# Scores of two heads in one ring slot, in the steps that have no tiles of maxima

## The chip, the cores and the metric

One core of a Trainium2 chip runs the whole program. The metric is the device time of one execution in microseconds (us), lower is better. A verdict compares runs of both kernels on the same chip.

## The reference

Eight sequences of 1024 tokens with 256 features pass through one transformer block: layer norm and modulation, attention with 16 heads of 16 features, then a feed-forward part with squared ReLU and a count of spikes over five steps. What matters here is the attention. Its scores pass through a softmax twice: first in blocks of 128 keys under a causal mask (a block that is wholly masked gives zeros), then, over all keys, on the results of the first.

```python
s = einsum('bhqd,bhkd->bhqk', q, k) / sqrt(16)
s = where(causal, s, -inf)                        # in blocks of 128 keys
e = exp(s - max(s, block));  probs = e / sum(e, block)   # masked blocks: 0
attn_probs = softmax(probs, axis=-1)              # over all 1024 keys
attn_out = einsum('bhqk,bhkd->bhqd', attn_probs, v)
```

## The kernel before

**Steps.** The scores are computed transposed, keys on the partitions. The lower triangle of key and query blocks of a head is cut into nine units of 512 columns (`UNITS`); a group of four heads passes through nine steps, one per unit, four groups make a batch of 36 steps, and 8 batches make 288 steps (`NUNIT`). Step n belongs to unit n % 9 and to place n % 36 of its batch. Units 1, 2 and 8 have two strips of keys, the others one.

**A step on TensorE** (`step` in the block of TensorE) goes through, in this order: the products with v of the unit seven steps back (line 799); the sums of e over a block of keys for the unit before (line 789); the spread of 1/sum over the partitions for the unit five steps back, in two ring slots (line 830); then the four heads' scores (lines 774 and 777, the second adds the causal mask), with other work put between them. In the steps of unit 0 the mixed products (lines 818 and 799) come ahead of the scores.

**Other work.** `FRONT` and `BACK` (and `FIRST`, `NEAR`, `LATE` at the ends) place the pieces of the next and the last batch by hand: transposes T1, T2 and AT (line 664), projections QK, V and O, the first feed-forward product F1 (line 719). `placed(n)` gives a step's two pieces; the first follows the first head's scores, the second the fourth head's. `QUANTA` places the second feed-forward product in quanta of two matmuls (line 731), in four places of a step. `tiles_of(n)` gives the tiles of block maxima (lines 749 and 752) of the next group: three in each step of units 1 to 6, none in those of units 7, 8 and 0, except at the very beginning. In unit 7 `turn_maxima` (line 762) transposes the maxima, and `outputs` (line 839) transposes the results of the group before.

**PSUM.** Four buffers take turns. Two score banks of 512 columns serve scores, pieces and the turned maxima in strict alternation (`score_slots`): whoever takes a bank waits until the one before it there has been read. Two ring slots of 1024 columns serve the spread 1/sums, the tiles of maxima and the outputs, alternating too (`RING_NO`): VectorE reads them all, and `ring_free` counts what it has freed.

**The other engines.** ScalarE takes each head's scores with one exponential of 512 columns (line 1042) into e, and five or six steps later takes the second exponential over 2048 columns (line 1047). VectorE multiplies e by the spread 1/sums, 1024 columns at a time (line 1181), takes maxima (line 1159) and splits them into two parts (lines 1173 and 1175), and does the layer norms' statistics (lines 1133 and 1139). GpSimd squares and splits. Each engine's order is written out; nothing is reordered at run time, and semaphores tie the engines together.

Of the kernel before, what the change touches and what calls it, by code (L numbers as in the profile page):

```python
# [54 lines left out]
LAG_R, LAG_E, LAG_P = 5, 6, 7  # L55
LAST = NUNIT + 14
# [7 lines left out]
for _h in range(QH):  # L64
# [17 lines left out]
FRONT = {(2, 1): ('T1', 0), (1, 0): ('T1', 1), (1, 1): ('T1', 2), (5, 0): ('T1', 3), (3, 1): ('QK', 0), (5, 1): ('QK', 1), (6, 0): ('QK', 2), (13, 0): ('QK', 3), (15, 0): ('QK', 4), (16, 1): ('QK', 5), (17, 0): ('QK', 6), (15, 1): ('V', 0), (19, 1): ('QK', 7), (24, 0): ('V', 1), (21, 1): ('V', 2), (29, 0): ('V', 3), (30, 0): ('BH', 0), (31, 0): ('BT', 0)}  # L82
BACK = {(8, 0): ('AT', 0), (8, 1): ('AT', 1), (9, 0): ('AT', 2), (12, 0): ('AT', 3), (10, 0): ('O', 0), (11, 0): ('O', 1), (12, 1): ('O', 2), (14, 0): ('O', 3), (18, 0): ('T2', 0), (18, 1): ('T2', 1), (20, 1): ('T2', 2), (24, 1): ('T2', 3), (19, 0): ('F1', 0), (20, 0): ('F1', 1), (21, 0): ('F1', 2), (23, 0): ('F1', 3), (26, 1): ('F1', 4), (27, 0): ('F1', 5), (27, 1): ('F1', 6), (28, 0): ('F1', 7), (32, 0): ('F1', 8), (32, 1): ('F1', 9), (33, 0): ('F1', 10), (35, 0): ('F1', 11), (38, 0): ('F1', 12), (39, 0): ('F1', 13), (40, 0): ('F1', 14), (40, 1): ('F1', 15)}
# [6 lines left out]
NEAR = {(39, 0): ("F1", 12), (39, 1): ("F1", 13), (41, 0): ("F1", 14), (41, 1): ("F1", 15)}  # L90
NEAR_QUANTA = {36: (0, 0, 0, 1), 37: (1, 1, 0, 1), 38: (2, 0, 3, 0), 42: (2, 2, 2, 2), 43: (2, 2, 2, 2)}
LATE = {(2, 0): ("AT", 0), (2, 1): ("AT", 1), (4, 0): ("O", 0), (4, 1): ("O", 1), (8, 0): ("AT", 2), (8, 1): ("AT", 3),
        (9, 0): ("T2", 0), (9, 1): ("T2", 1), (10, 0): ("O", 2), (10, 1): ("O", 3), (11, 0): ("F1", 0), (11, 1): ("F1", 1),
        (12, 0): ("F1", 2), (12, 1): ("F1", 3), (13, 0): ("F1", 4), (13, 1): ("F1", 5)}
# [4 lines left out]
    (2, 0): ("V", 0, 2), (2, 1): ("V", 0, 3), (6, 1): ("BH", 0, 0), (7, 1): ("BT", 0, 0),  # L99
    (10, 0): ("T1", 1, 0), (10, 1): ("T1", 1, 1), (11, 0): ("T1", 1, 2), (11, 1): ("T1", 1, 3),  # L100
# [16 lines left out]
def placed(n):  # L117

    out = [None, None]
    b, at = divmod(n, PERIOD)  # L120
    for k in range(2):
# [108 lines left out]

# [34 lines left out]

def score_slots():
# [3 lines left out]
    for n in range(LAST):  # L270
        p = placed(n)
        st = [("st", n, hh) for hh in range(QH)] if n < NUNIT else [None] * QH
        turn = ("turn", *turn_of(*turns(n))) if turns(n) else None
        begin = [p[0], st[0]] if piece_first(n) else [st[0], p[0]]
        steps.append([*begin, st[1], st[2], st[3], p[1], turn] if late_turn(n) else [*begin, st[1], turn, st[2], st[3], p[1]])
# [75 lines left out]
def build(nc, x, wqT, wkT, wvT, woT, bq, bk, bv, bo, wfcT, wprojT, cT, wmod, consts, out):  # L351
# [4 lines left out]
    with ExitStack() as ctx:  # L356
# [157 lines left out]

        block = ctx.enter_context(nc.Block())
# [3 lines left out]
        def _(sp):  # L519
# [18 lines left out]
            def load_stacks(g):  # L538
                b, f0 = g // NQ, QH * DK * (g % NQ)
                if g >= 2:  # L540
                    sp.wait_ge(st_ready, QH * NU * (g - 1))
# [101 lines left out]
        def _(pe):  # L643
# [32 lines left out]
            def piece(item):  # L676
# [25 lines left out]
                elif kind == "AT":  # L702
                    pe.wait_ge(ring_free, RING_NO["o", NQ * r + NQ - 1, n // NT if r == LB else 0] + 1)
# [61 lines left out]
            def scores(n, hh):  # L765
# [5 lines left out]
                slot = score_bank("st", n, hh)  # L771
# [6 lines left out]
                mm.then_inc(st_ready, 1)  # L778
# [101 lines left out]
            def step(n):  # L880
                first, second = placed(n)
# [13 lines left out]
                if piece_first(n) and first:  # L895
                    piece(first)
# [6 lines left out]
                if first and not piece_first(n):  # L903
                    piece(first)
                for item in single[0]:
                    quantum(n, *item)
                if n < NUNIT:
                    scores(n, 1)
                if turns(n) and not late_turn(n):
# [5 lines left out]
                if n < NUNIT:  # L915
                    scores(n, 2)
                if 1 in at:
# [7 lines left out]
                if second:  # L925
                    piece(second)
# [13 lines left out]
            def last_sums(c):  # L940

                pe.wait_ge(squared, 16 * LB + 4 * c + 4)
                pe.wait_ge(ring_free, len(RING_NO) - (1 if c == 0 else 0))
# [23 lines left out]
        def _(act):  # L967
# [68 lines left out]
            def first_exp(n, hh):  # L1036
# [4 lines left out]
                act.wait_ge(st_ready, QH * n + hh + 1)  # L1041
                act.activation(e[:, n % ES, hh, :], score[SCORE_SLOT["st", n, hh][0]][:, :], ACT.Exp, scale=DK ** -0.5).then_inc(e1_done, 1)  # L1042

            def second_exp(m):
                act.wait_ge(ring_free, RING_NO["r", m, 1] + 1)
# [9 lines left out]
            def sum_exp(t):  # L1055
                act.wait_ge(r_log, t + 1)
                act.activation(r_a[:, :], r_a[:, :], ACT.Exp, scale=-1.0).then_inc(r_exp, 1)

# [18 lines left out]
            def step(n):  # L1077
                b, s = divmod(n, PERIOD)
                first, second = placed(n)
# [8 lines left out]
                if piece_first(n) and first:  # L1088
                    take(first)
                if n < NUNIT:  # L1090
                    first_exp(n, 0)
                if first and not piece_first(n):
                    take(first)
                for item in sums_ended(n, 0):
                    take_sum(*item)
                if n < NUNIT:
                    first_exp(n, 1)
                if turns(n) and not late_turn(n):
                    take_turned(*turns(n))
                for item in sums_ended(n, 1):  # L1100
                    take_sum(*item)
                if n < NUNIT:
                    first_exp(n, 2)
                for item in sums_ended(n, 2):
                    take_sum(*item)
                if n < NUNIT:
                    first_exp(n, 3)
                if second:
                    take(second)
                for item in sums_ended(n, 3):  # L1110
                    take_sum(*item)
                if late_turn(n):
                    take_turned(*turns(n))
# [17 lines left out]
        def _(dve):  # L1131
# [34 lines left out]
            def split_maxima(g, k, blocks):  # L1166
# [3 lines left out]
                dve.wait_ge(ring_free, RING_NO["m", g, k] + 1)  # L1170
# [200 lines left out]
            def step(n):  # L1371
# [9 lines left out]
                first, second = placed(n)  # L1381
                if first and first[0] == "O":
                    take_output(first)
# [3 lines left out]
                if second and second[0] == "O":  # L1387
                    take_output(second)
# [177 lines left out]
```

## Time and profile before

| | |
|---|---|
| median of 3 runs | 2380.7 us (2380.19 to 2381.14) |
| the profiled execution | 2373.46 us |
| its span | 2371.6 us |
| TensorE, VectorE, ScalarE, GpSimd busy | 94%, 74%, 65%, 48% of the span |
| mean granted TensorE clock | 0.993 |

The span runs from the first instruction to the last; the rest of an execution's time lies around it. A busy share counts the time in which an engine has an instruction under way. TensorE's matmuls overlap: each is shown until its last result is written, some 0.16 us after the next has begun, so the starts of the instructions give their pace, and a wait that shows as idle time is about that much longer than shown. The releaser behind an idle time is the instruction whose semaphore ended it. The granted clock is the share of the full 2.4 GHz that TensorE got.

### The profile page before, as it was taken

The numbers are of one execution on the slowest core, as the hardware profiler recorded it, in microseconds if no ns is written. First come the engines' busy times: TensorE is split into PE (matmuls) and PEld (weight loads), VectorE is DVE, ScalarE is ACT, GpSimd is POOL, SyncE is SP. The second block draws the span as 40 slices with busy tenths as digits, with TensorE's granted clock in tenths as the row PEclk, the third lists the DMA queues.
The fourth block names the chain that finished last, engine by engine and source line by source line (L and its number), as shares of the span: only waits on it lengthen the run. The fifth ranks groups of instructions, "written<-read, shape, count | busy, mean of one in ns | idle before, by whom it ended". The sixth has DMA issues, their size and how long they took to land.

```text
span 2371.6 us, 46967 instructions
## 1 busy us (share of the span) xinstructions
PE 2220.5 (94%) x19324; PEld 1245.5 (53%) x19324; DVE 1750.9 (74%) x2113; ACT 1541.4 (65%) x2157; POOL 1137.5 (48%) x1070
## 2 busy tenths in 40 slices
PE   7889889999999999999999999999999999989988
PEld 4444344465545555455554555545554555545557
DVE  6787887768787676876778777776877767787456
ACT  2477676766667667675766766676666766667731
POOL 3153133545664456644666257653575544442630
PEclk8999999999999999999999999999999999999999
DMA  5233122211212113121133202231022211100000
GB/s 183 66 108 93 48 57 78 83 48 39 62 53 83 52 35 90 54 55 52 35 90 94 60 7 59 66 107 48 23 64 68 83 34 46 39 25 22 6 27 25
DMA packets 114066, 140.23 MB, mean 59 GB/s; under 512 B 8648, under 2 KB 86760, under 8 KB 113856
## 3 DMA queue, kind: packets, MB, share of 16 engines
q1 hardware_dynamic: 113856, 137.23, 20.4%
q8 instruction: 157, 2.57, 0.4%
q14 instruction: 53, 0.43, 0.1%
HBM read 74.26 MB, written 58.74 MB: 56 GB/s over the span
## 4 chain that ended last, share of the span: by engine, by line
PE 78%; DVE 9%; ACT 5%; POOL 4%; DMA 2%; issue 1%; SPq 0%; ACTq 0%; POOLq 0%
PE pv L799 11%; PE sums L789 9%; PE score L774 9%; PE ring L749 9%; PE score L719 8%; PE sums L731 8%; PE score L670 5%; PE score L687 4%; DVE e L1181 4%; PE ring L830 4%; DVE negmax L1159 3%; PE ring L752 2%; ACT e L1042 2%; PE score L777 2%; PE score L664 2%
## 5 line engine op out<-in xcount | busy, mean ns | idle before, releaser
L1042 ACT ACTIVATE e<-score 128x512 f32<-128x512 f32 x1152 | 672.2, 595 | 386.1 <-PE score L777 214.9
L1181 DVE TENSOR_TENSOR e<-ring,e 128x1024 f32<-128x1024 f32 x576 | 680.9, 1223 | 281.4 <-PE ring L830 281.0
L1159 DVE TENSOR_REDUCE negmax<-ring 128x8 f32<-128x1024 f32 x576 | 681.5, 1219 | 158.1 <-PE ring L752 147.2
L1047 ACT ACTIVATE e<-e 128x2048 f32<-128x2048 f32 x288 | 548.6, 1905 | 4.9 <-DVE e L1181 4.9
L774 PE MATMUL score<-q_st,k_st 112*128 112x512 bf16 (+3 forms) x1536 | 458.5, 330 | 56.3 <-ACT e L1042 23.7
L749 PE MATMUL ring<-k_st,q_st 96*128 96x512 bf16 (+3 forms) x1664 | 386.9, 317 | 38.8 <-DVE e L1181 18.4
L1486 POOL TENSOR_SCALAR r_p<-r_b,ab 128x256 bf16<-128x256 f32 x96 | 89.7, 934 | 548.7 <-DVE r_b L1187 548.7
L799 PE MATMUL pv<-e,v 128*17 128x512 f32 (+3 forms) x3072 | 311.4, 493 | 0.0
L789 PE MATMUL sums<-e,d_ones 128*32 128x256 f32 x4608 | 304.2, 382 | 1.5
L774 PEld LDWEIGHTS score<-q_st,k_st 112*128 112x128 bf16 x1536 | 147.8, 97 | 247.6 <-issue 120.7
L1465 POOL TENSOR_TENSOR gT<-gT 128x512 f32<-128x512 f32 x112 | 117.1, 1050 | 334.4 <-ACT gT L1015 334.4
L731 PE MATMUL sums<-w_proj,gT 128*128 128x256 f32 x896 | 259.4, 395 | 7.6 <-POOL gT L1465 3.7
L719 PE MATMUL score<-hT,w_fc 128*128 128x256 f32 x1024 | 244.3, 384 | 2.7 <-ACT e L1042 1.4
L789 PEld LDWEIGHTS sums<-e,d_ones 128*32 128x32 f32 x4608 | 147.3, 110 | 177.6 <-issue 92.2
L749 PEld LDWEIGHTS ring<-k_st,q_st 96*128 96x128 bf16 x1664 | 149.2, 98 | 146.3 <-DVE negmax L1159 42.2
L752 PE MATMUL ring<-mask_q,id_b 128*128 128x128 bf16 x1024 | 221.7, 221 | 0.0
L719 PEld LDWEIGHTS score<-hT,w_fc 128*128 128x128 f32 x1024 | 189.6, 190 | 33.3 <-ACT e L1042 6.3
L777 PE MATMUL score<-id_b,mask_q 128*128 128x128 bf16 x1024 | 192.3, 220 | 0.0
L731 PEld LDWEIGHTS sums<-w_proj,gT 128*128 128x128 f32 x896 | 148.4, 191 | 37.3 <-POOL gT L1465 6.5
L1477 POOL TENSOR_SCALAR below<-n 128x512 bf16<-128x512 f32 x104 | 154.9, 1490 | 7.4
L1015 ACT ACTIVATE gT<-score 128x512 f32<-128x512 f32 x112 | 66.9, 597 | 124.5 <-PE score L719 124.5
L752 PEld LDWEIGHTS ring<-mask_q,id_b 128*128 128x128 bf16 x1024 | 100.4, 98 | 53.3 <-issue 3.0
(148 smaller groups left out, 2600.2 us busy)
## 6 DMA issues: line engine op xcount, KB each, us to landing
q_st<-q_parts SPq DMA_DIRECT2D x31, 768.0 KB, 5.9
k_st<-k_parts SPq DMA_DIRECT2D x31, 768.0 KB, 8.7
q_parts<-qk_p SPq DMA_DIRECT2D x30, 384.0 KB, 2.6
k_parts<-qk_p SPq DMA_DIRECT2D x28, 384.0 KB, 2.6
x_in<-in_x SPq DMA_DIRECT2D x8, 1024.0 KB, 5.7
q_parts<-qk_p SPq DMA_DIRECT2D x30, 256.0 KB, 2.9
x_res<-in_x SPq DMA_DIRECT2D x30, 256.0 KB, 4.1
k_parts<-qk_p SPq DMA_DIRECT2D x28, 256.0 KB, 2.9
```

The lines of the kernel that those rows point to most:

```text
L719: mm = pe.matmul(ps[:, HALF * i:HALF * i + HALF], w_fc[:, k, P * f:P * f + P], (last_h if r == LB else hT2)[:, k, HALF * c:HALF * c + HALF ...
L731: mm = pe.matmul(sums[:, HALF:HALF + D], gT[:, f, P * i:P * i + P], w_proj[:, f, :], start=(n > NUNIT and f == 0), stop=(f == NF - 1), ski ...
L749: mm = pe.matmul(slot[:, c:stop], q, k_st[0:KROWS, g % 2, hh, c + shift:stop + shift], start=True, stop=not own, skip_group_check=True)
L752: mm = pe.matmul(slot[:, diag:diag + P], id_b[:, :], mask_q[:, :], start=False, stop=True, skip_group_check=True)
L774: mm = pe.matmul(slot[:, c:c + qb - qa], k_st[0:KROWS + MROWS, g % 2, hh, P * j:P * j + P], q_st[0:KROWS + MROWS, g % 2, hh, qa:qb], start ...
L777: mm = pe.matmul(slot[:, c:c + P], mask_q[:, :], id_b[:, :], start=False, stop=True, skip_group_check=True)
L789: mm = pe.matmul(sums[32 * hh:32 * hh + 32, 0:HALF], d_ones[:, 2 * TRI - 1 - row:2 * TRI + 31 - row], e[:, m % ES, hh, HALF * c:HALF * c + ...
L799: mm = pe.matmul(pv[32 * hh:32 * hh + VW, qa - at:qb - at], v1[:, b % 2, j, QH * g + hh, :], e[:, m % ES, hh, c:c + qb - qa], start=start, ...
L1042: act.activation(e[:, n % ES, hh, :], score[SCORE_SLOT["st", n, hh][0]][:, :], ACT.Exp, scale=DK ** -0.5).then_inc(e1_done, 1)
L1047: act.activation(v, v, ACT.Exp).then_inc(e2_done, 1)
L1159: dve.tensor_reduce(negmax[:, hh:hh + heads, at:at + NB // heads], slot[:, :].rearrange("p (h a n) -> p h a n", h=heads, n=P), AX_X, ALU.m ...
L1181: dve.tensor_tensor(v, ring[no % 2][:, :].rearrange("p (i n) -> p i n", i=2), v, ALU.mult).then_inc(ring_free, 1)
```

## The change

In the steps n for which `paired(n)` holds (units 0, 7 and 8, no tiles: 94 of the 288) the scores leave the score banks. They take two ring slots ("s", n, 0) and ("s", n, 1) behind the two of 1/sums, heads 0 and 1 in the halves of the first and heads 2 and 3 in those of the second, and ScalarE reads each slot with one exponential of 1024 columns. A ring slot whose last user were scores is waited for by `e1_done`, any other by `ring_free` as before, now counted by `FREE_NO` without the scores. The order within such a step is new: the first pieces and the first quanta go ahead of heads 0 and 1, the turned maxima and the middle quanta between the pairs, the rest behind. A step now has four places for pieces; what stood at the second place stands at the fourth in all tables, so other steps keep their order. `st_ready` counts only the other steps' scores (`ST_NO`), and SP's load of stacks waits by `scores_done`.

```diff
+PAIRED = (0, 7, 8)
...
+def paired(n):
+    return n % NU in PAIRED and n < NUNIT and not tiles_of(n)
...
     for _g, _k in tiles_of(_n):
         RING_NO["m", _g, _k] = len(RING_NO)
+    if paired(_n):
+        for _k in range(2):
+            RING_NO["s", _n, _k] = len(RING_NO)
     if turned_out(_n):
         RING_NO["o", turned_out(_n)[0], int(turned_out(_n)[1][0] > 0)] = len(RING_NO)
+RING_ITEM = list(RING_NO)
+FREE_NO = {item: k for k, item in enumerate(item for item in RING_ITEM if item[0] != "s")}
...
+        if paired(n):
+            steps.append([p[0], p[1], turn, p[2], p[3]])
+            continue
...
+        def scores_done(eng, n):
+            if paired(n):
+                eng.wait_ge(ring_ready, RING_NO["s", n, 1] + 1)
+            else:
+                eng.wait_ge(st_ready, ST_NO[n] + QH)
...
             def ring_slot(*item):
                 no = RING_NO[item]
-                if no >= 2:
-                    pe.wait_ge(ring_free, no - 1)
+                if no >= 2 and RING_ITEM[no - 2][0] == "s":
+                    _, n, pair = RING_ITEM[no - 2]
+                    pe.wait_ge(e1_done, QH * n + 2 * pair + 2)
+                elif no >= 2:
+                    pe.wait_ge(ring_free, FREE_NO[RING_ITEM[no - 2]] + 1)
                 return ring[no % 2]
...
-                slot = score_bank("st", n, hh)
+                if paired(n):
+                    if hh % 2 == 0:
+                        ring_slot("s", n, hh // 2)
+                    slot = ring[RING_NO["s", n, hh // 2] % 2][:, BANK * (hh % 2):BANK * (hh % 2) + BANK]
+                else:
+                    slot = score_bank("st", n, hh)
...
+                if paired(n):
+                    if p[1]:
+                        piece(p[1])
+                    for item in single[0]:
+                        quantum(n, *item)
+                    scores(n, 0)
+                    scores(n, 1)
+                    if turns(n):
+                        turn_maxima(*turns(n))
+                    for item in single[1]:
+                        quantum(n, *item)
+                    if p[2]:
+                        piece(p[2])
+                    for item in single[2]:
+                        quantum(n, *item)
+                    scores(n, 2)
+                    scores(n, 3)
+                    if p[3]:
+                        piece(p[3])
+                    if turned_out(n):
+                        outputs(*turned_out(n))
+                    for item in single[3]:
+                        quantum(n, *item)
+                    return
...
+            def paired_exp(n, pair):
+                if pair == 0:
+                    act.wait_ge(pv_done, blocks(n))
+                if pair == 0 and mixed(n):
+                    act.wait_ge(mixed_done, (n - LAG_P) // NU + 1)
+                no = RING_NO["s", n, pair]
+                act.wait_ge(ring_ready, no + 1)
+                act.activation(e[:, n % ES, 2 * pair:2 * pair + 2, :], ring[no % 2][:, :].rearrange("p (i n) -> p i n", i=2),
+                               ACT.Exp, scale=DK ** -0.5).then_inc(e1_done, 2)
...
+            def in_pairs(n, p):
+                for k in range(2):
+                    if p[k]:
+                        take(p[k])
+                for item in sums_ended(n, 0):
+                    take_sum(*item)
+                paired_exp(n, 0)
+                if turns(n):
+                    take_turned(*turns(n))
+                for item in sums_ended(n, 1):
+                    take_sum(*item)
+                if p[2]:
+                    take(p[2])
+                for item in sums_ended(n, 2):
+                    take_sum(*item)
+                paired_exp(n, 1)
+                if p[3]:
+                    take(p[3])
+                for item in sums_ended(n, 3):
+                    take_sum(*item)
```

## Rows read from the trace of the kernel before

**Rows 1.** The page, busy time, share of the span and instructions of an engine.

```profile
PE 2220.5 (94%) x19324; PEld 1245.5 (53%) x19324; DVE 1750.9 (74%) x2113; ACT 1541.4 (65%) x2157; POOL 1137.5 (48%) x1070
```

**Rows 2.** Groups by form: busy us, mean ns of one, idle us before with its releasers.

```profile
L1042 ACT ACTIVATE e<-score 128x512 f32<-128x512 f32 x1152 | 672.2, 595 | 386.1 <-PE score L777 214.9 <-PE score L774 148.7
L1047 ACT ACTIVATE e<-e 128x2048 f32<-128x2048 f32 x288 | 548.6, 1905 | 4.9 <-DVE e L1181 4.9
```

**Rows 3.** Windows: stretch, length, busy us of each engine, granted clock, DMA.

```profile
1208.72:1213.36 4.64, 4.64 (x37) 3.31 (x33) 3.00 (x3) 3.26 (x6) 4.29 (x6) 1.00 0.37 111
1215.55:1219.51 3.96, 3.96 (x34) 2.77 (x30) 2.35 (x2) 3.01 (x6) 0.00 (x0) 1.00 0.67 224
1221.27:1225.26 3.99, 3.37 (x30) 1.45 (x27) 3.11 (x4) 3.43 (x8) 0.57 (x1) 1.00 0.99 268
1276.15:1283.45 7.30, 4.94 (x32) 2.58 (x28) 5.24 (x15) 3.94 (x7) 2.52 (x3) 1.00 0.38 124
1285.65:1290.21 4.56, 3.54 (x24) 1.80 (x20) 4.33 (x9) 3.26 (x6) 2.85 (x3) 1.00 0.36 121
1292.31:1296.68 4.37, 3.69 (x33) 1.58 (x29) 3.26 (x5) 3.95 (x8) 4.37 (x4) 1.00 1.05 254
1345.86:1350.21 4.35, 4.28 (x34) 2.94 (x30) 2.66 (x3) 3.57 (x7) 0.00 (x0) 1.00 0.02 8
1352.41:1357.92 5.51, 5.51 (x39) 4.31 (x35) 2.36 (x2) 2.62 (x5) 0.00 (x0) 1.00 0.69 204
1359.67:1366.71 7.04, 6.20 (x40) 3.64 (x37) 3.11 (x4) 4.21 (x8) 3.42 (x6) 1.00 0.67 145
1419.49:1424.40 4.91, 4.29 (x34) 2.90 (x31) 4.16 (x13) 3.46 (x6) 4.65 (x4) 1.00 0.02 7
1426.59:1432.22 5.63, 5.44 (x37) 3.74 (x33) 5.39 (x8) 3.55 (x6) 5.38 (x5) 1.00 0.06 9
1433.97:1437.44 3.47, 2.83 (x27) 1.06 (x23) 3.27 (x4) 2.62 (x6) 3.31 (x4) 1.00 1.07 248
```

**Rows 4.** Timeline of VectorE: start, length, line, operation, tiles, count, idle before.

```profile
1209.16 2.56 DVE L1181 TENSOR_TENSOR e<-ring,e 128x1024 f32<-128x1024 f32 x2
...
1215.64 2.35 DVE L1181 TENSOR_TENSOR e<-ring,e 128x1024 f32<-128x1024 f32 x2 [1.10 <-PE ring L830]
...
1279.15 2.33 DVE L1181 TENSOR_TENSOR e<-ring,e 128x1024 f32<-128x1024 f32 x2
...
1345.96 2.56 DVE L1181 TENSOR_TENSOR e<-ring,e 128x1024 f32<-128x1024 f32 x2
...
1421.37 2.32 DVE L1181 TENSOR_TENSOR e<-ring,e 128x1024 f32<-128x1024 f32 x2
```

**Rows 5.** Timeline of TensorE, step 16 of the batch.

```profile
1276.44 0.38 PE L774 MATMUL score<-q_st,k_st 112*128 112x512 bf16 x1
...
1278.40 0.61 PE L762 MATMUL score<-id_b,maxp 128*64 128x128 bf16 x8 [1.52 <-DVE maxp L1175]
1278.93 0.39 PE L774 MATMUL score<-q_st,k_st 112*128 112x512 bf16 x1
...
1280.67 1.98 PE L687 MATMUL score<-hT,w_q 128*128 128x512 f32 x4
```

**Rows 6.** Timeline of TensorE, first scores of steps 9, 27 and 0.

```profile
1222.61 0.39 PE L774 MATMUL score<-q_st,k_st 112*128 112x512 bf16 x1
...
1362.36 0.39 PE L774 MATMUL score<-q_st,k_st 112*128 112x512 bf16 x1
...
1434.73 0.39 PE L774 MATMUL score<-q_st,k_st 112*128 112x512 bf16 x1
```

**Rows 7.** Timeline of TensorE, a tile of maxima in batch 7.

```profile
2113.71 0.23 PE L749 MATMUL ring<-k_st,q_st 96*128 96x128 bf16 x1 [1.91 <-DVE e L1181]
```

**Rows 8.** Windows of batch 7 and of the last steps.

```profile
2115.00:2121.00 6.00, 5.64 (x33) 1.76 (x31) 5.85 (x11) 2.69 (x3) 3.19 (x4) 0.50 0.00 0
2258.20:2261.40 3.20, 3.20 (x26) 0.94 (x24) 0.69 (x1) 0.00 (x0) 3.04 (x3) 0.50 0.00 0
```

More of the change, by code:

```diff
@@ L117, in placed @@
 def placed(n):
-    out = [None, None]
+    out = [None] * 4
     b, at = divmod(n, PERIOD)
-    for k in range(2):
+    for k in range(4):
         if b == 0 and (at, k) in FIRST:
@@ L263, in piece_first @@
     return mixed(n) or n == max(BEGIN_AT) + 1
+ST_NO = [QH * sum(not paired(k) for k in range(n)) for n in range(NUNIT)]
 def score_slots():
@@ L271, in score_slots @@
         p = placed(n)
-        st = [("st", n, hh) for hh in range(QH)] if n < NUNIT else [None] * QH
+        st = [("st", n, hh) for hh in range(QH)] if n < NUNIT and not paired(n) else [None] * QH
         turn = ("turn", *turn_of(*turns(n))) if turns(n) else None
+        if paired(n):
+            steps.append([p[0], p[1], turn, p[2], p[3]])
+            continue
         begin = [p[0], st[0]] if piece_first(n) else [st[0], p[0]]
-        steps.append([*begin, st[1], st[2], st[3], p[1], turn] if late_turn(n) else [*begin, st[1], turn, st[2], st[3], p[1]])
+        steps.append([*begin, st[1], p[1], *([] if late_turn(n) else [turn]), st[2], p[2], st[3], p[3], *([turn] if late_turn(n) else [])])
     steps.append(TAIL)
@@ L880, in step @@
             def step(n):
-                first, second = placed(n)
+                p = placed(n)
                 single = quanta(n)
@@ L894, in step @@
                     one_over_sums(n - LAG_R, 1)
-                if piece_first(n) and first:
-                    piece(first)
+                if (piece_first(n) or paired(n)) and p[0]:
+                    piece(p[0])
                 if mixed(n):
                     mixed_products(n - LAG_P)
+                if paired(n):
[22 more added lines that the diff above has]
+                    return
                 if -1 in at:
@@ L902, in step @@
                     scores(n, 0)
-                if first and not piece_first(n):
-                    piece(first)
+                if p[0] and not piece_first(n):
+                    piece(p[0])
                 for item in single[0]:
@@ L908, in step @@
                     scores(n, 1)
+                if p[1]:
+                    piece(p[1])
                 if turns(n) and not late_turn(n):
@@ L916, in step @@
                     scores(n, 2)
+                if p[2]:
+                    piece(p[2])
                 if 1 in at:
@@ L924, in step @@
                     maxima(*at[2])
-                if second:
-                    piece(second)
+                if p[3]:
+                    piece(p[3])
                 if 3 in at:
@@ L1078, in step @@
                 b, s = divmod(n, PERIOD)
-                first, second = placed(n)
+                p = placed(n)
                 t = n // TRI - 1
@@ L1087, in step @@
                     sum_exp(t)
[L1088 to L1113, printed above, removed]
+                if paired(n):
+                    in_pairs(n, p)
+                else:
+                    by_heads(n, p)
                 if s == 34 and b + 2 < B:
@@ L1380, in step @@
                     invert(t)
-                first, second = placed(n)
-                if first and first[0] == "O":
-                    take_output(first)
+                p = placed(n)
+                for item in p[:2]:
+                    if item and item[0] == "O":
+                        take_output(item)
                 tiles = tiles_of(n)
@@ L1386, in step @@
                     maxima(g, k)
-                if second and second[0] == "O":
-                    take_output(second)
+                for item in p[2:]:
+                    if item and item[0] == "O":
+                        take_output(item)
                 if turned_out(n):
```

66 lines of the change are left out of this document (51 added, 15 removed).

## The prediction

> **What bounds the kernel now.** I read the page's busy times first: TensorE is busy for 94% of the span, no other engine over three quarters [rows 1]. So an edit pays only as far as it shortens TensorE's order of work or its waits; a shorter time of ScalarE by itself pays nothing. Next the windows: one for each kind of step that the change touches, from the end of the two matmul groups that spread 1/sum over the partitions (line 830; I call that moment R) to the first product of the next step [rows 3]. Length less busy time is TensorE's idle time there, 59.73 - 52.71 = 7.0 us for the twelve steps of a batch. That is all the change can win, some 56 us in eight batches, and only if it brings no wait of its own. The windows stand in the order of the steps 7, 8, 9, 16, 17, 18, 25, 26, 27, 34, 35 and 0 of a batch of 36. Last the timeline, for who uses the ring at that moment.
>
> **What the change does to the order.** Before, the scores of a step start at R, in banks of their own, and the ring's two slots are then in the hands of VectorE, which multiplies them into e (line 1181). Now the first two heads' scores need the slot of the first multiply, the last two that of the second. Row by row, VectorE is done with the two slots after R: 1.31 and 2.44 us in steps where it is idle when R comes (step 8, the window that starts at 1215.55); 1.87 and 3.00 in step 7; 4.20 and 5.33 in step 16; 1.53 and 2.66 in step 25; 3.07 and 4.20 in step 34 [rows 4]. The first multiply ends 1.13 us before the second, since each row holds two. The steps 7, 16, 25 and 34 are late because VectorE first splits the maxima (lines 1173, 1175), and in 16 and 34 ends the statistics of a layer norm as well. That work hangs on the last tile of the step before, so it doesn't move. What I call the fill is what TensorE has to do between R and the first scores: its first piece, its first quanta, and in steps 9, 18, 27 and 0 the mixed products. I add 0.06 us from VectorE's end to TensorE's start (the matmul at 2113.71 starts that long after the first of two multiplies) [rows 7].
>
> **Prices.** A head of scores takes 0.29 us (1276.15 to 1276.44), so a pair 0.56, and 0.66 in the steps with two strips (six blocks of 128 columns against five). The transposes of the maxima take 0.53, a QK piece with the outputs behind it 2.78, the QK piece alone some 1.8 [rows 5]. The mixed products take 0.76, with a piece of transposes ahead 1.34, with an F1 piece ahead 2.69, so the piece is 0.58 or 1.93 [rows 6]. A quantum is 0.48: the first window is fully busy for 4.64 us and holds four heads, the transposes, the outputs (0.96) and four quanta.
>
> **Step by step**, in us from R. The length before is the window's [rows 3].
> Step 7: fill 0.96, scores at 1.93, 2.49; transposes and two quanta to 3.98; second pair to 4.54; outputs 0.96: 5.5 against 4.64, +0.9.
> Step 8: fill 1.0, scores at 1.37 to 2.03, quantum, second pair at 2.51 to 3.17, tail 1.0: 4.2 against 3.96, +0.2.
> Step 9: fill 1.34, pairs at 1.37 and 2.5, to 3.06, tail 0.6: 3.65 against 3.99, -0.35.
> Step 16: no fill. Scores at 4.26 to 4.82, transposes to 5.35, second pair at 5.39 to 5.95, tail 2.78: 8.7 against 7.30, +1.4. TensorE stands still for 4.2 us in one piece.
> Step 17: the QK piece is the fill, pairs at 1.8 and 2.5, to 3.17. The four scores no longer wait for that piece's bank, and 1.4 us goes. But the next step's sums wait for the exponentials: ScalarE takes the QK piece first (two passes, at least 0.6 each), then twice 1.03, so until 5.3; behind the sums 1.31 (the 2.19 from 1213.36 to 1215.55, less 0.88 of products) makes 6.6 against 6.66 (1285.65 to 1292.31): -0.1.
> Step 18: as step 9, -0.3. Step 25: fill 0.48, scores at 1.59, 2.15, transposes and two quanta to 3.6, 4.2, outputs: 5.2 against 4.35, +0.8.
> Step 26: no fill. Scores at 1.37 to 2.03, five quanta to 4.4, pair, F1 1.93: about 6.9 against 5.51, +1.3.
> Step 27: fill 2.69, by when both slots are free; pairs to 3.8, F1: 5.7 against 7.04, -1.3.
> Step 34: fill 0.48, scores at 3.13, 3.7, transposes and two quanta 5.2, 5.75, outputs: 6.7 against 4.91, +1.8; one pause of 2.6 us.
> Step 35: fill 1.93, then no wait: -0.5. Step 0: fill 0.76, scores at 1.37 and 2.5, to 3.06, quantum and 0.1: +0.2.
> The sum is +4.1 us a batch. Batches 0, 1 and 7 have other fills (no quanta or no pieces); by the same working they give +2, +4 and +3. With five full ones: 20.5 + 9 = **+30 us** of waits.
>
> The exponential of 1024 columns isn't in the trace. Between 0.595 at 512 and 1.905 at 2048 columns [rows 2] the line gives 1.03; the other end is two of the old ones, 1.19. It lies beside TensorE's work except in step 17, where two of them add up: 0.3 us a batch at most, 2 us in all. The shorter ScalarE time itself (94 steps by 0.3 us) is hidden behind TensorE. That the QK, F1 and transposed pieces no longer share banks with scores in these steps is in the sums above; it is the whole gain of steps 17 and 27. SP's load of the next stacks now hangs on the ring instead of the scores, at the same point of the order; it costs nothing as long as step 8's second pair ends within 0.3 us of before.
>
> **The clock.** The pauses have a second price. The trace shows a pause of 1.91 us before 2113.71, and from 2115.00 to 2121.00 a granted clock of 0.50, the lower level of 1.2 GHz; one more such stretch, of 3.2 us, comes among the last steps; the pause of 1.52 us in step 16 of today leaves the clock at 1.00 in its window [rows 3, 5, 7, 8]. New pauses of 1.9 us and over come in step 16 of batches 1 to 6 (4.2 us), in step 34 of batches 0 to 6 (2.4 to 2.6), and in steps 8 and 43 of the kernel, where nothing fills: fifteen. A stretch of 3.2 us or a little more at half clock costs 1.7 us, fifteen: **+25 us**. Bounds: none, if the clock holds; 3.0 each (6 us at half clock), so 45. I take the short stretch because TensorE is busy all through it (3.20 of 3.20 us), and the work behind the new pauses is as dense.
>
> The Trainium skill (TensorE: Matmul & The Clock Gate, section "Why this matters for your kernels") warns against idle gaps between bursts of matmuls, since after one the engine runs at half clock. The trace agrees: 0.50 behind 1.91 us. Without that effect the sum would be +30 alone.
>
> **The sum.** The profiled execution took 2373.5 us; 2373.5 + 30 + 25 = 2428.5. The median of the runs is 7.2 us above the profiled one, so **2435 us**.
>
> **Rivals.**
> *Waits alone.* The clock holds at 1.00 through pauses of 4 us, or falls only in the few longest: 2380.7 + 30 = 2411. For it: 1.5 us pauses leave it alone. Against: the stretch behind 1.91. Chance 0.22.
> *Long stretches.* Each fall lasts 6 us: 2380.7 + 30 + 45 = 2456. Chance 0.07.
> *Faster.* The chain through the score banks (scores, exponential, scores) is what the change takes away, and if VectorE gives the slots back before TensorE comes, only the steps that gain are left. The place is the first scores of a pair step; it decides at a multiply that ends less than the fill after R. Without the losses of 7, 8, 16, 25, 26, 34 and 0 a batch gains 2.6 us: 2360. For it: five steps of twelve are so already. Against: in 16, 26 and 34 there is little or no fill. Chance 0.08.
> *No change.* Later steps with idle time of their own take the delay back: VectorE's maxima wait less where TensorE comes later. Seven steps in twelve lose, and little idle time is left in steps 1 to 6 to take it back. Chance 0.03, 2381.
> The forecast itself, waits and short stretches, has 0.60.
>
> **How the numbers follow.** Slower by over 0.2% (5 us, about what can be told from no change) holds in the forecast and the first two rivals: 0.89; within 0.2%: 0.03; faster 0.08. The range goes from under the waits alone, 2404, to just under the long stretches, 2452.
>
> **What would show it.** Right: TensorE's first score of step 16 waits on line 1181 for about 4 us, and the scores' waits on ScalarE's exponentials are gone; idle time of TensorE before scores grows from VectorE; windows of step 27 are 1.3 us shorter; about fifteen stretches at 0.50, and a mean clock near 0.98. The 1024-column exponential shows 1.03. Wrong: a clock of 0.99 (then the waits alone), first scores that start before the multiply ends, or a step 34 that isn't longer.

## The result, and the profile after

The changed kernel takes 2444.8 us (median of 4 runs, 2440.3 to 2447.8) against 2380.4 before (2376.3 to 2381.1): a ratio of 1.0276, 95% interval 1.0259 to 1.0293. The profiled execution took 2440.3 us against 2373.5, so 66.9 us more; 2435 were forecast, 2404 to 2452 the range.

The page of the changed kernel: its first line, the busy times, and the engines' shares of the chain that ended last.

```profile
span 2438.5 us, 46842 instructions
PE 2234.1 (92%) x19324; PEld 1260.8 (52%) x19324; DVE 1757.5 (72%) x2113; ACT 1518.1 (62%) x1969; POOL 1138.6 (47%) x1070
PE 73%; DVE 21%; ACT 2%; issue 2%; DMA 1%; POOL 1%; SPq 0%; ACTq 0%; POOLq 0%
```

ScalarE did what the change wanted, 23 us less work than in [rows 1]. It stands off the path: TensorE has the same matmuls, 14 us more of busy time (they ran slower) and more idle time. VectorE's share of the chain was 9% before and is 21% now, though its work is the same. Who waits for it stands in the list of waits (waiter, releaser, us in total, times, longest):

```profile
PE ring L811 <- DVE e L1290: 95.8, 90, 4.2
...
PE sums L829 <- ACT e L1119: 12.7, 17, 1.3
```

Line 811 is the scores' matmul (774 before), line 1290 the multiply (1181 before). Before, no score waited for a multiply; now 90 pauses add up to 95.8 us. The scores' waits on exponentials went from 23.7 us (52 times) to 5.6 (15 times); what is left is in steps without pairs. The second row is a wait that is new as well, of the sums for the joint exponential. The groups by form give the exponentials their price:

```profile
L1110 ACT ACTIVATE e<-score 128x512 f32<-128x512 f32 x776 | 458.8, 595 | 292.1 <-PE score L811 149.8 <-PE score L814 132.2
...
L1119 ACT ACTIVATE e<-ring 128x1024 f32<-128x1024 f32 x188 | 190.9, 1024 | 203.2 <-PE ring L814 200.2
```

1.024 us where 1.03 was estimated. The windows of [rows 3], in the same order and from R to the next step's first product (stretch, length, busy us of TensorE, weight loads, VectorE, ScalarE and GpSimd, granted clock, DMA):

```profile
1242.98:1248.65 5.67, 4.84 (x37) 3.30 (x33) 3.03 (x3) 2.63 (x3) 5.24 (x7) 1.00 0.33 94
1250.84:1255.05 4.21, 3.92 (x35) 2.73 (x31) 2.36 (x2) 2.33 (x3) 0.00 (x0) 1.00 0.49 169
1256.80:1260.53 3.73, 3.25 (x30) 1.52 (x27) 3.11 (x4) 3.35 (x6) 0.31 (x1) 1.00 1.07 230
1311.71:1322.83 11.12, 6.95 (x32) 3.65 (x28) 5.22 (x15) 3.78 (x5) 2.50 (x3) 0.69 0.25 84
1325.02:1328.31 3.29, 3.29 (x24) 1.85 (x20) 3.05 (x7) 1.81 (x4) 1.95 (x2) 1.00 0.11 38
1331.53:1336.34 4.81, 3.24 (x32) 1.64 (x28) 4.34 (x6) 3.17 (x6) 4.81 (x5) 1.00 1.07 248
1385.53:1390.83 5.30, 4.41 (x35) 2.93 (x31) 2.65 (x3) 2.73 (x4) 0.00 (x0) 1.00 0.00 0
1393.02:1399.85 6.83, 5.52 (x38) 4.36 (x35) 2.35 (x2) 2.43 (x3) 0.00 (x0) 1.00 0.55 169
1401.61:1407.28 5.67, 5.67 (x40) 3.69 (x37) 3.11 (x4) 3.97 (x6) 2.14 (x4) 1.00 0.78 176
1460.06:1468.54 8.48, 6.05 (x34) 3.91 (x31) 4.17 (x13) 2.81 (x3) 7.96 (x7) 0.80 0.03 12
1470.73:1475.85 5.12, 5.12 (x37) 3.98 (x33) 4.88 (x9) 2.54 (x4) 2.70 (x3) 1.00 0.02 3
1477.61:1481.65 4.04, 2.73 (x27) 1.11 (x23) 3.52 (x5) 2.35 (x5) 3.96 (x4) 1.00 1.07 258
```

Lengths against the forecast, in us:

| step | before | forecast | after |
|---|---|---|---|
| 7 | 4.64 | 5.5 | 5.67 |
| 8 | 3.96 | 4.2 | 4.21 |
| 9 | 3.99 | 3.65 | 3.73 |
| 16 | 7.30 | 8.7 and the clock | 11.12 at 0.69 |
| 17 | 4.56 | 3.17 | 3.29 |
| 18 | 4.37 | 4.05 | 4.81 |
| 25 | 4.35 | 5.2 | 5.30 |
| 26 | 5.51 | 6.9 | 6.83 |
| 27 | 7.04 | 5.7 | 5.67 |
| 34 | 4.91 | 6.7 and the clock | 8.48 at 0.80 |
| 35 | 5.63 | 5.1 | 5.12 |
| 0 | 3.47 | 3.7 | 4.04 |

Step 17 was forecast to give its gain back before the next R: 6.6 us from R to R (1325.02 to 1331.53), against 6.66 before. It took 6.51.

Step 16 on TensorE's timeline (the changed kernel), and then the passage from step 17 to 18:

```profile
1315.94 0.61 PE L811 MATMUL ring<-q_st,k_st 112*128 112x512 bf16 x1 [4.17 <-DVE e L1290]
1316.34 0.31 PE L814 MATMUL ring<-id_b,mask_q 128*128 128x128 bf16 x1
...
1330.19 1.07 PE L829 MATMUL sums<-e,d_ones 128*32 128x256 f32 x16 [1.25 <-ACT e L1119]
...
1332.40 0.63 PE L696 MATMUL score<-id_f,x_in 128*128 128x128 f32 x4 [0.80 <-DVE x_in L1390]
```

The first score stands 4.17 us in one piece, and the matmul behind it takes 0.61 us instead of 0.38: the clock is down to half. A window that starts in the pause:

```profile
1314.30:1321.00 6.70, 5.05 (x19) 2.51 (x20) 2.72 (x10) 3.02 (x3) 0.07 (x1) 0.50 0.38 124
```

In step 18 there is a wait that nobody forecast: the transposes wait 0.80 us for VectorE's layer norm (line 1390). The layer norm's four instructions, and the first GpSimd instruction that splits a QK piece, before (two rows) and after (two rows):

```profile
1288.81 3.15 DVE L1281 TENSOR_SCALAR x_in<-x_res,mv,rstd 128x256 f32<-128x256 f32 x4
1289.31 1.25 POOL L1452 TENSOR_TENSOR qk_p<-qk_f,qk_p 128x512 bf16<-128x512 f32 x1 [1.63 <-ACT qk_p L993]
...
1328.19 4.06 DVE L1390 TENSOR_SCALAR x_in<-x_res,mv,rstd 128x256 f32<-128x256 f32 x4
1328.39 1.24 POOL L1563 TENSOR_TENSOR qk_p<-qk_f,qk_p 128x512 bf16<-128x512 f32 x1 [1.33 <-ACT qk_p L1061]
```

The same four instructions start 3.2 us after R of step 17 in both, but take 4.06 us instead of 3.15. One by one they are of two lengths: 0.41 us where GpSimd is idle when they start, 1.25 to 1.32 where it has one of its QK instructions under way. The QK piece now goes ahead of the scores, so GpSimd starts 3.4 us after R instead of 3.7, and three of the four are slow instead of two.

The mean clock fell from 0.993 to 0.982: (1 - 0.982) x 2438.5 - (1 - 0.993) x 2371.6 = 27 us of full speed lost. The other 40 us are put down to waits; that is the remainder, and the first experiment measures it another way.

### The profile page after: what moved, and what is told of

The parts are those of the page before. It is cut to its first block, busy times and chain, and to the rows that moved or that the text cites. A ratio compares the mean times of both kernels' runs of the same rounds, so it can differ in the third digit from the quotient of the medians.

```text
span 2438.5 us, 46842 instructions
## 1 busy us (share of the span) xinstructions
PE 2234.1 (92%) x19324; PEld 1260.8 (52%) x19324; DVE 1757.5 (72%) x2113; ACT 1518.1 (62%) x1969; POOL 1138.6 (47%) x1070
## 4 chain that ended last, share of the span: by engine, by line
PE 73%; DVE 21%; ACT 2%; issue 2%; DMA 1%; POOL 1%; SPq 0%; ACTq 0%; POOLq 0%
PE pv L839 9%; DVE e L1290 9%; PE sums L829 9%; PE ring L781 8%; PE score L751 8%; PE sums L763 7%; PE score L811 6%; DVE negmax L1268 5%; PE score L702 5%; PE score L719 4%; PE ring L870 3%; PE ring L811 3%; PE ring L784 2%; DVE maxp L1284 2%; DVE x_in L1390 1%
## 5 line engine op out<-in xcount | busy, mean ns | idle before, releaser
L1110 ACT ACTIVATE e<-score 128x512 f32<-128x512 f32 x776 | 458.8, 595 | 292.1 <-PE score L811 149.8
L811 PE MATMUL score<-q_st,k_st 112*128 112x512 bf16 (+3 forms) x1032 | 310.9, 330 | 17.8 <-ACT qk_p L1061 11.2
L1119 ACT ACTIVATE e<-ring 128x1024 f32<-128x1024 f32 x188 | 190.9, 1024 | 203.2 <-PE ring L814 200.2
L811 PE MATMUL ring<-q_st,k_st 112*128 112x384 bf16 (+1 forms) x504 | 140.0, 345 | 96.3 <-DVE e L1290 95.8
L811 PEld LDWEIGHTS score<-q_st,k_st 112*128 112x128 bf16 x1032 | 99.0, 97 | 126.7 <-issue 50.1
L1083 ACT ACTIVATE gT<-score 128x512 f32<-128x512 f32 x112 | 66.9, 597 | 115.7 <-PE score L751 115.7
```

The source lines that it names most:

```text
L811: mm = pe.matmul(slot[:, c:c + qb - qa], k_st[0:KROWS + MROWS, g % 2, hh, P * j:P * j + P], q_st[0:KROWS + MROWS, g % 2, hh, qa:qb], start ...
L1119: act.activation(e[:, n % ES, 2 * pair:2 * pair + 2, :], ring[no % 2][:, :].rearrange("p (i n) -> p i n", i=2), ACT.Exp, scale=DK ** -0.5) ...
```

## Experiments

Each was timed beside the kernel before; ratios carry 95% intervals. The theory: the first pair waits for VectorE's multiply in the ring, the pauses bring the clock down, and nothing is won where ScalarE wasn't on the path. Its rivals: the ring wait costs alike everywhere, the order within the step costs, the clock is no matter.

**The clock by itself.** The pauses stay, and useless matmuls run in them.

```diff
+FILL = {8: 16, 43: 11, **{36 * b + 16: 17 for b in range(1, 7)}, **{36 * b + 34: 9 for b in range(7)}}
...
+                    for _ in range(FILL.get(n, 0)):
+                        pe.matmul(score_bank("turn", *turn_of(*turns(n))), id_b[:, :], mask_q[:, 0:1].to_broadcast([P, BANK]), start=True, stop=True, skip_group_check=True)
                     scores(n, 0)
```

> The changed kernel, with matmuls of no use (512 columns, into the score bank that the turned maxima overwrite) in the fifteen pauses of step 16, step 34 and the kernel's steps 8 and 43, just shorter than each pause: 16, 11, 17 and 9 of them. Theory (waits and clock): the waits stay, but the stretches at half clock behind these pauses go, 58 us of stretch, so about 29 us: some 2416 us, mean clock 0.99. Rival (the clock costs nothing here, the waits on VectorE are all of it): the same time as the changed kernel, 2445 us, or a little more where the fill reaches past the pause.

Measured: 2421.9 us, ratio 1.0188 (1.0164 to 1.0211), 23 us under the changed kernel (21 by the two ratios), mean clock 0.990. Doing more work made it faster. Its windows of steps 16 and 34:

```profile
1303.11:1311.88 8.77, 8.39 (x50) 4.21 (x46) 5.23 (x15) 3.60 (x5) 2.51 (x3) 1.00 0.28 95
1450.03:1456.87 6.84, 6.37 (x43) 3.81 (x39) 4.17 (x13) 2.62 (x3) 6.49 (x5) 1.00 0.00 0
```

At a clock of 1.00 step 16 takes 8.77 us (8.7 forecast) and step 34 takes 6.84 (6.7). So the two terms of the sum come apart: these steps' waits are as worked out, and the rest of 11.12 and 8.48 is the clock. The clock didn't get back to 0.993, since it fell at smaller pauses instead: in step 18 of three batches, behind waits of 1.25 and 0.80 us, and in step 33 of batch 0. The runs of the kernel before beside it had a clock of 0.988 to 0.993, the filled ones 0.989 to 0.992, and still 45 us lie between the medians. So the waits cost 40 to 45 us.

**Where the loss sits.** `PAIRED = (0, 8)`, then `PAIRED = (7,)`.

> Pairs only in the steps of units 8 and 0; unit 7 goes by single heads, as before. Theory (VectorE is late in unit 7, since it splits the maxima there): what is left is small, some +7 us against before by the step lengths of the two traces, 2388 us, no new stretch at half clock, mean clock 0.993. Rival (the ring wait costs in every step alike): two thirds of the loss stay, 2423 us.

> Pairs only in the steps of unit 7. Theory: nearly the whole loss, waits of 1, 4, 1 and 2.5 us and the half clock behind the long ones: some 2380 + 57 = 2437 us, clock 0.982. Rival (equal cost per step): a third of the loss, 2402 us.

Measured: without unit 7 2402.9 us, 1.0108 (1.0086 to 1.0129), clock 0.984; unit 7 alone 2430.0 us, 1.0221 (1.0200 to 1.0243), clock 0.981. One step in three makes most of the loss, which excludes the rival. Unit 7 alone was 7 us under the expectation. The other was 15 us over it. Its step 16, which goes by single heads as before and has the same pause of 1.52 us before the turned maxima, shows why; a row of TensorE's timeline and the window of the step:

```profile
1295.20 0.61 PE L794 MATMUL score<-id_b,maxp 128*64 128x128 bf16 x8 [1.52 <-DVE maxp L1284]
```

```profile
1292.96:1301.95 8.99, 6.63 (x33) 3.33 (x29) 5.23 (x15) 4.27 (x7) 2.51 (x3) 0.81 0.31 103
```

8.99 us at a clock of 0.81 against 7.30 at 1.00 in [rows 3]. The same pause left the clock alone in the profile of the kernel before and brought it down here, in five of batches 1 to 6; in four of them the clock fell in step 18 too. Nor does the kernel decide it alone. With pairs in unit 7 only, step 34 has the same pause of 2.4 us in every batch from 0 to 5; behind it the clock fell in batches 1, 3 and 5 and held in 0, 2 and 4. Two windows of that profile, behind the pause in batches 3 and 4:

```profile
1168.50:1171.50 3.00, 3.00 (x12) 2.00 (x11) 0.00 (x0) 1.52 (x3) 2.83 (x3) 0.50 0.06 22
1461.50:1464.50 3.00, 3.00 (x38) 1.95 (x40) 0.97 (x2) 2.72 (x6) 2.83 (x3) 1.00 0.06 22
```

These two kernels also show what step 35 owes to the change. Its window without unit 7 in pairs (step 35 in pairs), then with unit 7 alone (step 35 by single heads), and last its wait in the kernel before:

```profile
1446.23:1451.87 5.64, 5.39 (x37) 3.89 (x33) 5.40 (x8) 2.89 (x4) 5.38 (x5) 1.00 0.09 12
...
1465.58:1470.76 5.18, 5.18 (x38) 3.83 (x34) 4.94 (x10) 3.46 (x7) 4.03 (x4) 1.00 0.01 3
...
1431.59 0.70 PE L731 MATMUL sums<-w_proj,gT 128*128 128x256 f32 x2 [0.19 <-POOL gT L1465]
```

In pairs it takes 5.64 us, as before (5.63); untouched, behind a late step 34, it takes 5.18. Its gain is a wait for GpSimd that is over by the time a delayed TensorE comes, and not the pairs' doing.

**VectorE's order.** The maxima split behind the multiplies, and turned behind the fourth head, from group 2 on.

```diff
                     times_inverse(n - LAG_R, 1)
+                if last_turn(n):
+                    split_maxima(turns(n)[0], len(TILES) - 1, range(NB))
...
                     scores(n, 2)
                     scores(n, 3)
+                    if last_turn(n):
+                        turn_maxima(*turns(n))
```

> The changed kernel, but from group 2 on VectorE splits the maxima behind the two multiplies of the step instead of ahead of them, and TensorE turns them behind the fourth head. Theory (the split ahead of the multiplies makes the pause): the first pair of unit 7 starts some 1.4 us (steps 7 and 25) to 2.4 us (steps 16 and 34, where the layer norm's statistics stay ahead) after the last spread of 1/sums; the half-clock stretches go, and 5 to 6 us a batch are saved by the waits and 3 to 4 by the clock: some 2385 us. Rival (the pause is the ring's order, not VectorE's work): no change, 2445 us.

Measured: 2447.7 us, 1.0292 (1.0262 to 1.0322): nothing won. Yet the pause was cut: the waits for the multiply fell to 61.9 us, and step 16 took 7.58 us from R where the clock held, in batches 4 and 5. In the other four of batches 1 to 6 the clock fell in it all the same, behind a pause of 1.58 us. Step 16 of batch 4, and a part of step 16 of batch 3:

```profile
1323.93:1331.51 7.58, 4.84 (x32) 2.63 (x28) 4.08 (x12) 3.81 (x5) 2.35 (x3) 1.00 0.33 110
1034.00:1039.00 5.00, 4.76 (x15) 2.27 (x14) 0.27 (x1) 2.03 (x2) 0.00 (x0) 0.50 0.42 143
```

More time came back elsewhere, two steps behind step 34, in the profile of this kernel (VectorE and TensorE around step 0 of a batch):

```profile
1481.55 3.62 DVE L1399 TENSOR_SCALAR x_in<-x_in,mv,rstd 128x256 f32<-128x256 f32 x4
1485.09 0.68 DVE L1315 TENSOR_TENSOR o_t<-pv,suf 128x512 f32<-128x512 f32 x1
...
1485.83 0.40 PE L863 MATMUL pv<-mask_q,id_b 128*17 128x512 bf16 x4 [2.16 <-DVE o_t L1315]
```

Four instructions of a layer norm hold VectorE for 3.62 us (2.77 in the changed kernel); its next instruction frees the product bank, and TensorE waits 2.16 us, long enough for the clock to fall in five of seven batches. Steps 7 and 25 grew as well, since the turned maxima now wait for a split that comes later. The theory was right that the split ahead of the multiplies makes the pause, and wrong that the half clock goes with it and that the time is won: VectorE's work was moved, not shortened. Which part of the return is the layer norm, which the clock, I haven't separated.

**Only where the fill is long.** Pairs in step 27 of batches 1 to 7 alone (`return n % PERIOD in PAIRED and PERIOD <= n < NUNIT`, `PAIRED = (27,)`).

> Pairs in one step of a batch alone: step 27 (unit 0, behind an F1 piece) of batches 1 to 7. Theory (where the fill outlasts VectorE's two multiplies, the pair costs no wait and saves the wait on the exponential): 1.36 us a batch less, 9.5 us, so 0.996 of before (2367 of 2377). Rival (the saving is taken back one step later): 1.000.

Measured: 2372.2 us, ratio 0.9978 (0.9967 to 0.9989). Half of what was expected. Windows of its steps 16 and 27:

```profile
1281.80:1290.45 8.65, 6.34 (x33) 3.11 (x29) 5.24 (x15) 3.95 (x7) 2.52 (x3) 0.80 0.33 109
1366.65:1372.33 5.68, 5.68 (x41) 3.70 (x37) 3.11 (x4) 3.98 (x6) 2.15 (x4) 1.00 0.79 183
```

Step 27 gives its 1.36 us (7.04 to 5.68); step 16, which isn't touched, loses 1.35 (7.30 to 8.65) to the clock, in batches 1 to 6 of this execution. It was the slowest of the ten, with a mean clock of 0.987; the others had 0.988 to 0.991, the 22 runs of the kernel before 0.989 to 0.994. So one profile of each kernel overstates the difference, but the lower clock is there on average. In this profile the clock also fell three times in batch 0 (from 131.9, 179.7 and 299.2 us), which has no pairs in this kernel either; the profile of the kernel before has no fall there.

**Step 17 too, ScalarE's pairs ahead of the QK piece.**

```diff
+                late = n % PERIOD == 17
                 for k in range(2):
-                    if p[k]:
+                    if p[k] and not late:
                         take(p[k])
...
                 paired_exp(n, 1)
+                for k in range(2):
+                    if p[k] and late:
+                        take(p[k])
```

> Steps 17 and 27 of batches 1 to 7, and in step 17 ScalarE takes the two exponentials of 1024 columns ahead of the QK piece's two passes. Theory (in step 17 the next sums wait for ScalarE's order): step 17 is 1.3 us shorter, the next step's sums wait only 0.75 us instead of 1.25, so 0.5 us a batch on top of step 27's 1.36: 13 us, 0.9945 of before. Rival (VectorE's layer norm, a fixed 4 us behind step 17, holds step 18 whatever ScalarE does): as step 27 alone, 0.996 or a little above.

Measured: 2379.5 us, 1.0017 (1.0002 to 1.0032): worse than step 27 alone. Theory and rival both fall. The layer norm isn't fixed: with ScalarE's QK passes later, GpSimd starts later too, and the same four instructions take 1.38 us, and the transposes of step 18 don't wait for them. Its layer norm and the first GpSimd instruction of the QK piece:

```profile
1297.73 1.38 DVE L1394 TENSOR_SCALAR x_in<-x_res,mv,rstd 128x256 f32<-128x256 f32 x4
1300.51 1.16 POOL L1567 TENSOR_TENSOR qk_p<-qk_f,qk_p 128x512 bf16<-128x512 f32 x1 [4.84 <-ACT qk_p L1061]
```

The sums waited 0.85 us, near the 0.75 expected, but ScalarE had its two QK passes, the second exponential and the logarithms still before it, and in step 18 TensorE stood for that, a row of its timeline:

```profile
1303.76 0.38 PE L811 MATMUL score<-q_st,k_st 112*128 112x512 bf16 x1 [1.30 <-ACT hT L1043]
```

Step 18 took 5.29 us from R against 4.37 before. In three batches the clock fell in it as well, and the mean clock of the runs was 0.981 to 0.990.

**The joint exponential by itself.** The changed kernel, each ring slot read by two exponentials of 512 columns.

```diff
-                act.activation(e[:, n % ES, 2 * pair:2 * pair + 2, :], ring[no % 2][:, :].rearrange("p (i n) -> p i n", i=2),
-                               ACT.Exp, scale=DK ** -0.5).then_inc(e1_done, 2)
+                for i in range(2):
+                    act.activation(e[:, n % ES, 2 * pair + i, :], ring[no % 2][:, BANK * i:BANK * i + BANK], ACT.Exp, scale=DK ** -0.5).then_inc(e1_done, 1)
```

> The changed kernel with each pair in the ring taken by two exponentials of 512 columns instead of one of 1024. Theory (the ring costs, the joint exponential gives next to nothing): two take 1.19 us against 1.02 and show only where sums wait for them, steps 1, 10 and 18 of a batch: 0.17 to 0.35 us each, 4 to 6 us in all, 2450 us. Rival (the joint exponential is a real part of the time): 94 steps by two pairs by 0.17 us = 32 us more, 2477 us.

Measured: 2445.5 us, 1.0282 (1.0269 to 1.0296), against 1.0276 for the changed kernel: the joint exponential is worth nothing that shows, less even than the 4 to 6 us expected.

**The order by itself.** The new order within the steps, scores in the score banks, exponentials of 512.

```diff
+        if in_order(n):
+            steps.append([p[0], p[1], st[0], st[1], turn, p[2], st[2], st[3], p[3]])
...
+            def paired_exp(n, pair):
+                first_exp(n, 2 * pair)
+                first_exp(n, 2 * pair + 1)
```

> The new order within the 94 steps (first pieces and quanta ahead of heads 0 and 1, the rest between the pairs and behind), but the scores stay in the score banks with exponentials of 512 columns. Theory (the ring's slots make the loss): near the kernel before, 2380 to 2392 us, since the banks let the first two heads start at once and the third waits for an exponential as before; mean clock 0.99. Rival (the order is what costs): most of the loss, 2430 us and over.

Measured: 2403.9 us, 1.0107 (1.0092 to 1.0121), clock 0.987. So the order costs 27 us without the ring, its falls of the clock included, more than the theory allowed for and less than the rival. Its windows of steps 7, 16 and 26:

```profile
1223.48:1228.70 5.22, 4.75 (x36) 3.35 (x32) 3.02 (x3) 3.15 (x6) 4.79 (x7) 1.00 0.35 99
1291.95:1300.65 8.70, 6.38 (x32) 3.16 (x28) 5.23 (x15) 3.95 (x7) 2.51 (x3) 0.80 0.33 108
1370.70:1376.72 6.02, 5.67 (x39) 4.39 (x35) 2.36 (x2) 2.52 (x5) 0.00 (x0) 1.00 0.75 210
```

Against 4.64, 7.30 and 5.51 before. With two heads side by side in banks of one head each, the turned maxima (step 7) and the F1 piece (step 26) must wait for an exponential that fills once covered; in step 16 it is the clock once more. In the changed kernel the ring spares these bank waits and puts its own, longer ones in their place, so the costs of order and ring don't add.

**Taking the pause of step 16 away.** Three kernels: step 27 in pairs with five useless matmuls in the pause; the kernel before with the maxima turned at the end of steps 16 and 34, VectorE's order as it was; both step 27 and the late turn.

```diff
+def last_turn(n):
+    return late_turn(n) or bool(turns(n)) and n > PERIOD and n % PERIOD in (16, 34)
...
-                if late_turn(n):
+                if last_turn(n):
                     turn_maxima(*turns(n))
```

> Pairs in step 27 alone, and five matmuls of no use (512 columns) in the pause of step 16 before the turned maxima, which so far lasts 1.5 us. Theory (in the kernel with step 27 alone each batch gains 1.36 us there and loses 1.34 us to the clock in step 16): the fall of the clock in step 16 goes, and the 1.36 us a batch show: 0.996 of before or under. Rival (the clock falls there for another reason than the pause): 0.998, as without the fill.

> The kernel before with the maxima turned at the end of steps 16 and 34 of batches 1 to 6, no pairs anywhere. Theory: the pause of step 16 goes, 2.2 us a batch with step 34, some 14 us: 0.994 of before. Rival (layer norm as above): 0.999 to 1.000.

> Pairs in step 27 of batches 1 to 7 alone, and in steps 16 and 34 of these batches the maxima are turned at the end of the step, behind the outputs, where VectorE's split is long done. Theory: step 27 gives 1.36 us a batch; step 16 loses its pause of 1.5 us before the turn, and with it the fall of the clock, and keeps the waits on exponentials: about 1.6 us; step 34 0.6 us. 3.5 us in each of six batches, 21 to 25 us, 0.990 of before. Rival (VectorE's layer norm behind steps 16 and 34, whose length is fixed, comes too late for the next mixed products, and the time returns in steps 18 and 0): 0.997, as with step 27 alone.

Measured: step 27 with the pause filled 2370.0 us, 0.9957 (0.9944 to 0.9971); late turn alone 2366.8, 0.9945 (0.9933 to 0.9958); **both 2358.9, 0.9910 (0.9896 to 0.9924)**, the fastest of all and 20.6 us under the 2379.4 of its neighbour runs. The interval of the filled kernel touches that of step 27 alone (0.9967 to 0.9989), so its trace must tell what the fill does; step 16 of it:

```profile
1276.86:1284.33 7.47, 5.93 (x36) 2.99 (x34) 5.24 (x15) 3.95 (x7) 2.51 (x3) 1.00 0.37 122
```

7.47 us at 1.00 instead of 8.65 at 0.80: the fall is gone from step 16, in all of batches 1 to 6, and the fill costs 0.17 us itself. Windows of steps 16, 27 and 34 of the last:

```profile
1266.80:1272.64 5.84, 5.13 (x33) 2.50 (x29) 5.67 (x17) 3.44 (x6) 2.68 (x4) 1.00 0.39 131
1348.85:1354.52 5.67, 5.67 (x40) 3.70 (x36) 3.11 (x4) 3.97 (x6) 2.13 (x4) 1.00 0.79 182
1407.30:1412.02 4.72, 4.33 (x34) 2.94 (x30) 4.59 (x15) 2.39 (x4) 4.46 (x4) 1.00 0.00 0
```

Step 16 went from 7.30 to 5.84, step 27 from 7.04 to 5.67, step 34 from 4.91 to 4.72. Here QK and outputs run while VectorE splits; the turned maxima come last, and their reader is two steps away. The feared return in steps 18 and 0 didn't come: only step 34's 0.19 is lost again in step 35, which is 0.27 longer, so turning late pays in step 16 alone. From R to R that is 1.4 us a batch, some 9 us of the 13 that the late turn gained; the rest would fit a clock that falls in some runs of the kernel before (0.988 to 0.992, against 0.990 to 0.993), which no trace shows.

## Why the prediction was right

**The bound.** ScalarE's saving (23 us of busy time) bought nothing; two exponentials in place of one gave the same time (1.0282 and 1.0276 of before). As forecast.

**The wait.** The first pair waits for the multiply of its slot, 4.17 us in step 16 against 4.2 forecast, and ten of the twelve kinds of step came within 0.2 us of the forecast where the clock was whole, steps 16 and 34 with the pauses filled. Steps 18 and 0 are the two that didn't.

**The size of the waits.** +30 us forecast, 40 to 45 measured. The term that was too small is what happens behind a step that got shorter or ends in a joint exponential. Step 18 was forecast at -0.3 and came at +0.44 (4.37 to 4.81), step 0 at +0.2 and came at +0.57: two different things. At step 0 the layer norm ends when it did, and a TensorE that is 0.5 us sooner in step 35 waits for it. At step 18 TensorE is only 0.15 us sooner, and the layer norm ends 0.9 us later, since it runs beside GpSimd for longer; the experiment with step 17, in which it takes 1.38 us and the wait is gone, bears this out. And steps 1 and 10, which I didn't look at, wait 0.28 us each for step 0's and 9's last exponential. Against the forecast that is 0.7 + 0.4 + 0.6 = 1.7 us a batch, up to 13 us in eight batches, where 10 to 15 are missing; the batches at the ends have less of it. I said that VectorE's lateness "doesn't move"; that holds of the split and the statistics, not of the layer norm, whose length depends on when GpSimd works beside it.

**The clock.** +25 us forecast, 27 from the mean clocks, 23 from the filled pauses. The fifteen places were right but for step 43 of the kernel, whose pause of 2.9 us left the clock whole. The rule I read from the rows (1.9 us or more) was too firm. Pauses of 1.52 and of 2.4 us bring the clock down in one place and not in another, between kernels and between the batches of one execution, so for pauses of 1 to 3 us a trace shows what happened, not what must. My two bounds, none and 3.0 us each, held, but of fourteen stretches four were long: 6.8 us in step 16 of batches 3 to 6, the others 3.4. (So are the two short ones near the end of the kernel before, where I named one, of 3.2.) The forecast had one fall too many and four too short; these errors work against each other, and that the sum came this close is in part luck.

**What I gave to the wrong cause.** The prediction charged all to the ring. The order alone costs 27 us in banks; only the ring makes its losses of another kind. The forecast held because each step was added up as it would run, not by parts of the edit. Step 35 came out at its 5.1 us for another reason than the one given: the pairs gave it nothing, and it gained because step 34 was late.

**Rivals.** Waits alone (2411): refuted by the stretches at 0.50 behind fourteen of the fifteen pauses and by the filled kernel, which keeps its waits and is 23 us faster. Long stretches (2456): four of the fourteen were long, and the time lies between. No change (2381): little came back, the 0.5 us of step 35 a batch. Faster (2360): of the five steps that were to gain, step 27 alone does (9.22 to 7.86 us from R to R). Step 9 gives its 0.26 us back to the next sums, step 17 all but 0.15, step 18 loses, and step 35's gain isn't the pairs'. Where step 27 stands alone the kernel is indeed faster, 0.9978.

## What to carry to other kernels

An engine's spare buffer is only spare while its reader is done with it: before moving work into another ring, take from the trace when that ring's slots are freed, step by step, and compare with what the waiting engine can do until then. Count an engine's fixed work again when its neighbours move: the layer norm here took 1.38, 3.15 or 4.06 us by what GpSimd did beside it. In a kernel that keeps one engine busy to 94%, a shorter pause can pay twice, since a longer one may also cost the clock; move work with distant readers into it or behind it. And test a change step by step: one step of twelve gained by the pairs, and with the turned maxima moved it made the fastest version.

## What the runs showed of the hardware

The granted clock fell to 0.50 behind pauses of 4.2 us, and also behind two short ones in a row (1.25 and 0.80 us, in step 18 with the long pauses filled). In the steps treated here it stayed there for 3.4 or 6.8 us with dense work behind. Whether a pause of 1.5 us does it differs between kernels whose step is the same, and one of 2.4 us did it in every other batch of one execution; what decides it stays open. In the profile of the kernel with pairs in step 27 alone this took back 1.35 of 1.36 us a batch. Matmuls without use in the pauses of the changed kernel gave 23 us. At half clock a matmul of 512 columns is shown at 0.61 us instead of 0.38.

A normalising instruction of VectorE (128x256) behind step 17 took 0.41 us where GpSimd was idle when it started, and 1.25 to 1.32 us where GpSimd worked on the QK parts beside it.
